# Full-array transposes of the probabilities, and the scores between the output runs, in a two-layer graph network

## The reference

```python
x = layernorm(x + (adj @ x) @ weight + bias)              # layer 0, for every batch
q, k, v = split(x @ w_qkv)                                # layer 1: 8 heads of 64
attn = softmax(where(adj == 0, -inf, q @ k.T * 64**-0.5))
o = (attn @ v) @ w_proj + b_proj
x = layernorm(x + o + layernorm(o) * gamma + beta)
```

## Time and profile before

| | before |
|---|---|
| three runs, median | 3365.83 us |
| profiled execution, its own time | 3366.38 us |
| its span in the profile | 3364.6 us |
| layer 0 | start to some 780 us |
| layer 1, fill in every group | some 840 to 3290 us |
| last pairs and last projection | some 3290 us to the end |
| TensorE busy in the span | 3308.5 us (98%) |

### The profile page before, as it was taken

The page is one execution under the profiler, slowest core; times in us unless marked ns, Lnnn a source line. Parts: engine busy times, 40 slices in busy tenths (PEclk is TensorE's granted clock), DMA queues, the critical chain, the costliest instruction groups (busy, mean ns, idle before and its releaser), DMA issues. The chain is left out here.

```text
span 3364.6 us, 88016 instructions
## 1 busy us (share of the span) xinstructions
PE 3308.5 (98%) x31792; PEld 2923.1 (87%) x31792; DVE 2623.7 (78%) x6434; ACT 2229.6 (66%) x4634; POOL 1997.1 (59%) x2690
## 2 busy tenths in 40 slices
PE   8999999998999999999999999999999999999996
PEld 6888888886899998889899899899999899998894
DVE  7666666665788888888888888888888888888887
ACT  4444444444677777777777777777777777777775
POOL 4555556552466666666666666666666666666666
PEclk8999999998999999999999999999999999999998
DMA  5565555653011111111122211111111111111210
GB/s 188 174 195 168 186 187 172 190 180 102 27 52 51 55 54 51 51 55 51 51 63 66 66 51 51 51 51 51 51 54 54 51 51 54 51 51 53 70 59 32
DMA packets 345217, 279.62 MB, mean 83 GB/s; under 512 B 13713, under 2 KB 275857, under 8 KB 344977
## 3 DMA queue, kind: packets, MB, share of 16 engines
q1 hardware_dynamic: 344976, 275.83, 27.0%
HBM read 141.56 MB, written 134.22 MB: 82 GB/s over the span
## 5 line engine op out<-in xcount | busy, mean ns | idle before, releaser
L1126 ACT ACTIVATE pt_hi<-bank 128x512 fp32r<-128x512 f32 x1024 | 557.0, 596 | 546.3 <-PE bank L835 533.9
L1119 ACT ACTIVATE probs<-probs,bias_row 128x512 f32<-128x512 f32 x1024 | 731.7, 721 | 44.7 <-DVE bias_row L1239 43.6
L1259 DVE TENSOR_TENSOR pt_lo<-bank,pt_hi 128x512 fp32r<-128x512 f32 x1024 | 658.0, 684 | 44.0 <-PE bank L858 34.3
L721 POOL TENSOR_SCALAR probs<-probs,inv_sums 128x480 f32<-128x480 f32 (+1 forms) x1024 | 685.3, 682 | 0.0
L1239 DVE CUSTOM_DVE_ANT_0 probs<-bank,mask_bias 128x512 f32<-128x512 f32 x1024 | 661.9, 684 | 9.7 <-PE bank L819 5.8
L718 POOL TENSOR_TENSOR probs<-probs,inv_sums 128x32 f32<-128x32 f32 x512 | 122.7, 240 | 730.4 <-DVE inv_sums L1248 730.3
L872 PE MATMUL bank<-x_lo,w_hi 64*128 64x512 f32 x1024 | 403.3, 394 | 0.0
L870 PE MATMUL bank<-x_lo,w_hi 64*128 64x512 f32 x1024 | 403.3, 394 | 0.0
L872 PE MATMUL bank<-x_hi,w_hi 64*128 64x512 f32 x992 | 403.2, 406 | 0.0
L870 PE MATMUL bank<-x_hi,w_hi 64*128 64x512 f32 x992 | 401.6, 405 | 0.0
L835 PEld LDWEIGHTS bank<-ident,probs 64*128 64x128 f32 x8192 | 362.9, 139 | 40.8 <-issue 4.9
(11 more groups left out here) (139 smaller groups left out, 10847.2 us busy)
## 6 DMA issues: line engine op xcount, KB each, us to landing
x_in<-in_x_dram SPq DMA_DIRECT2D x32, 1024.0 KB, 5.2
u_beta_rows<-ub SPq DMA_DIRECT2D x32, 1024.0 KB, 4.4
ut_hi<-ut_hi_sb SPq DMA_DIRECT2D x128, 256.0 KB, 4.1
ut_lo<-ut_lo_sb SPq DMA_DIRECT2D x128, 256.0 KB, 3.8
x_lo<-ut_lo SPq DMA_DIRECT2D x128, 256.0 KB, 4.7
out_dram<-o SPq DMA_DIRECT2D x128, 256.0 KB, 3.2
ub_row<-u_beta_rows SPq DMA_DIRECT2D x124, 256.0 KB, 2.7
x_hi<-ut_hi SPq DMA_DIRECT2D x124, 256.0 KB, 4.4
```

The source lines that it names most:

```text
L721: pool.tensor_scalar(probs[:, k % 2, a, cols], probs[:, k % 2, a, cols], inv_sums[:, k % 4, a:a + 1], 0.0, ALU.mult, ALU.add)\
L1119: act.activation(probs[:, k % 2, a, :], probs[:, k % 2, a, :], ACT.Exp, bias=bias_row[:, k % 4, a:a + 1], scale=-1.0, accum_out=sums[:, k ...
L1126: act.activation(turned_into(pt_hi, k, i), turned(i), ACT.Copy).then_inc(pthi_made, 1)
L1259: dve.tensor_tensor(turned_into(pt_lo, k, i), turned(i), f32(turned_into(pt_hi, k, i)), ALU.subtract).then_inc(ptlo_made, 1)
```

## The change

The transposes take all 128 rows: one for each head and each block of 128 keys, eight in a turn. Each takes 128 x 128 of `probs` as the weights and the 128 x 128 identity as the moving operand. Head a now lands in bank a, so that the views of the banks change, and ACT waits for each bank by itself. In the fourth step eight couples of fill stand ahead of run 0, and the scores stand between the two runs. The first step has six couples of fill at its end, and the second step 18 in place of 20. The number of fill couples in a group stays 48.

```diff
             def turned(i):
-                return t_bank[i][:].rearrange("p (a m n) -> p a m n", a=2, m=T)
+                return t_bank[i][:].rearrange("p (m n) -> p m n", m=T)
             def turned_into(rows, k, i):
-                first = k % T * P + i * HEAD
-                return rows[:, :, :, first:first + HEAD]
+                return rows[:, i, :, k % T * P:(k % T + 1) * P]
...
                     for a in range(2):
                         for m in range(T):
-                            for i, h in enumerate((TOP, BOTTOM)):
-                                cols = slice((a * T + m) * HEAD, (a * T + m + 1) * HEAD)
-                                last = pe.transpose(t_bank[i][:, cols], probs[h, k % 2, a, m * P:(m + 1) * P],
-                                                    ident[h, h])
-                                if a == 1 and m == T - 1:
-                                    last.then_inc(probs_turned, 1)
+                            cols = slice(m * P, (m + 1) * P)
+                            last = pe.transpose(t_bank[a][:, cols], probs[:, k % 2, a, cols], ident[:])
+                            if m == T - 1:
+                                last.then_inc(probs_turned, 1)
...
first_step:
-                        fill_and_wait(group, 12, 4, k + 1)
+                        fill_and_wait(group, 12, 6, k + 1)
second_step:
-                            fill(group, 16, 10)
+                            fill(group, 18, 9)
                         scores_ahead(k)
-                        fill_and_wait(group, 26, 10, k + 1)
+                        fill_and_wait(group, 27, 9, k + 1)
last_step:
-                            fill(group + 1, 0, 6)
+                            fill(group + 1, 0, 8)
...
                         attend_v(b, group, pt_hi, 0)
-                        if more_fill:
-                            fill(group + 1, 6, 2)
+
+                        scores_ahead(k, turn_next=True)
                         attend_v(b, group, pt_hi, 1)
-                        scores_ahead(k, turn_next=True)
...
                 def pt_hi_part(b, k):
-                    act.wait_ge(probs_turned, b * 32 + (2 * k + 2))
                     for i in range(2):
+                        act.wait_ge(probs_turned, b * 32 + (2 * k + i + 1))
                         act.activation(turned_into(pt_hi, k, i), turned(i), ACT.Copy).then_inc(pthi_made, 1)
```

## The result

The changed kernel took 3669.25 us, median of four runs (3668.71 to 3669.60), against 3365.68 us for the kernel of before: ratio 1.0905, 95% interval 1.0889 to 1.0921, so 304 us slower. I had predicted 3696 us (3540 to 3775), 330 us slower.

What follows compares the result with a forecast made beforehand. TensorE's own stream was taken to set the time of layer 1. 3366.4 us, plus 343 for 512 longer turns, minus 13 for the stall ahead of run 0, gave 3696 us, range 3540 to 3775 us.

Steps and rivals of the forecast that it cites:

- What bounds the kernel: TensorE's own stream sets layer 1's time; whatever the change adds to this stream it adds to the time.
- The full-array transpose: In a turn: 0.11 us each, against 0.061 for a half-array couple; eight take 0.88 us, 0.39 more.
- Rival B: Full-array transposes go at a half-array couple's pace, 0.061 us: 3496 us; chance 0.06.
- The change of mode: Ahead of and behind each turn, going half to full array and back costs 0.28 us together.
- Rival A: The 0.28 us for the change of mode is hidden behind matmuls in flight: 3553 us; chance 0.12.
- Rival E: The change of mode costs twice as much, 0.56 us: 3839 us; chance 0.05.
- Number of turns: All 512 turns counted at 0.67 us more each, the few without fill at the end included: +343 us.
- Eight fills ahead of run 0: Two more fill couples than today's six hide the 0.11 us that TensorE's stream loses there: -13 us.
- ACT's earlier start: ACT may begin its first copy after four transposes, which helps only where TensorE waits: 0.
- The fill moved to the first step: Fill moved from the second step to the first, and no fill less: 0.
- The scores between the runs: Fourth step: same work, two waits 0.92 us earlier; the longer turn hides the earlier wait: 0.
- Rival D: Fourth step, cheap turn: ready_to_turn waits for pt_lo, some 0.3 us in three of four groups: 3381 us; chance 0.03.

Runs made afterwards that it cites:

- experiment 1: The full-array transposes alone on the kernel of before, TensorE's order as before: 3682.7 us, ratio 1.0945.
- experiment 6: The kernel of before with one full-array transpose more at the head of every turn: 3577.8 us, ratio 1.0633.
- experiment 7: The kernel of before with layer 0's turns made by 16 full-array transposes instead of 32 half-array ones: 3377.7 us, ratio 1.0038.
- experiment 3: The kernel of before with the changed order, half-array transposes, and the wait for the next turn at run 1's last couple: 3340.7 us, ratio 0.9927.
- experiment 5: The kernel of before with fill moved between first and second step alone (4, 10, 10 couples become 6, 9, 9): 3356.2 us, ratio 0.9973.
- experiment 2: The changed kernel's order alone, with the half-array transposes of the kernel of before: 3382.0 us, ratio 1.0051.
- experiment 4: The changed kernel with the wait for the next turn moved to the last couple of run 1: 3670.0 us, ratio 1.0907.

## Why the prediction was right, and where it was off

**What bounds the kernel: right.** Experiments 1, 6 and 7 add to TensorE's stream, and the time grows by what the timeline shows, within 20 us: 504 x 0.67 = 338 us for 318 measured, 504 x 0.41 = 207 for 213, and 31 x 0.41 = 12.7 for 12.7. Of the 20 us too much in the first, 14 are the stall ahead of run 0, which goes.

**The full-array transpose: right.** I took 0.11 us from the last records of line 152; it is 0.109. Rival B (0.061 us) is refuted. The 56 ns of the Trainium skill (TensorE: Matmul & The Clock Gate, Back-to-back issue gap) do not hold for these fp32 transposes either. The page gives that figure for a matmul by itself, and some 81 ns for a stream of weight loads and matmuls of 128 columns, which I had not set beside it; the measured 109 ns is above both.

**The change of mode: right.** It was taken from layer 0, in the other direction: a turn with 1.23 us in all. It has 1.68 - 0.46 = 1.22. Experiments 6 and 7 show the price apart from the transposes (0.30 and 0.35 us for two changes). Rivals A and E are refuted. The Trainium skill (TensorEngine Tiling (Array Packing), Key Properties) says that such a change drains TensorE; the trace agrees, with 0.32 us from the last matmul to the first transpose.

**Number of turns: 5 us too much.** I took all 512. The last eight steps have no fill; from turn 504 to turn 511 the kernel of before takes 35.7 us (3296.9 to 3332.6) and the changed one 35.3 (3600.5 to 3635.8). I had reasoned that a longer turn on the chain of waits counts in full, which would be 4.7 us over these seven distances. With the transposes alone (experiment 1) the same turns take 38.2 us (3611.9 to 3650.1), so the longer turn costs 2.5 us there, about half of that, and the new order takes it back. That ACT starts in the middle of the turn would explain the half; no run tests it.

**Eight fills ahead of run 0: the number right, the cause not needed.** The stall goes, and 13 us is its size. With the short turn the two couples hide it: experiment 3, which has them, is 15 us faster than experiment 5, which hasn't. But experiment 1 has six couples as before and no stall. With the full-array transposes ACT's copies start no later than before, while run 0 comes 0.67 us later. I had put ACT's earlier start at nothing; in this kernel it does the work, together with the longer turn, and the two couples add nothing to it. Where ACT waits for the end of the turn the stall stays, although the turn is 0.41 us longer (experiment 6). So the -13 us came out right in part by luck: the same stall is covered twice, and the cover that I named is not the one that was needed.

**The fill moved to the first step: wrong, at nothing.** I wrote that no fill less means 0. With the short turn it takes a stall of 0.09 us out of each group, 9 us measured (experiment 5); with the long turn half of that stall is gone already (experiment 1). The row for it, the idle time of line 870's weight loads, lay beside the one for run 0 that I read.

**The scores between the runs: right for this turn.** I said that the earlier wait is hidden by the longer turn alone. Experiments 2 to 4 show just this. Rival D's price, 3381 us with a short turn, was measured as 3382, and this nearness is luck. The place and the three groups of four were right, but the gap is 0.43 us and not 0.3 (some 12 us too little), and I had not counted the second stall that the order removes (9 us too much).

**The sum.** 504 x 0.67 = +338, less 14 for run 0, less 9 for the first step, gives 315; measured are 304. The rest of 11 us I can only point at. Four steps take 19.82 us before and 22.24 us after, so 2.42 more; 4 x 0.67 - 0.11 - 0.09 = 2.48, and 0.06 us a group are left, 8 us in all. In the changed kernel the couples are down to 0.227 us after five behind most turns, before after some ten. No run here tests what does this, so this part of the sum stays open. The range that I gave for my own case, 3640 to 3760, was added up too narrow: both of its lower bounds together give 3624, both upper ones 3773.

## What to carry to other kernels

Where TensorE has no gap, count the moving columns and the changes between half-array and full-array instructions, not the instructions: two half-array transposes at the same time move half as many columns in turn as one full-array one, and a short burst in another mode pays for the drain twice. A reordering has to be read by each wait that moves with it; here one wait, four couples too early, turned a gain of 24 us into a loss of 17. And a cover such as "the longer turn hides it" belongs to the combination: test each half of a change by itself.

## What the hardware showed that I had not expected

A stall of a tenth of a microsecond on TensorE is not in its matmul rows at all: the records are 0.39 us long and 0.23 us apart, and so they bridge it. The idle time of the weight loads with "issue" as its cause showed both stalls, at once and counted (123 and 104 times). Not every such row is a stall of the order, though. In the changed kernel the change into full-array mode stands there as well: from 860 to 3590 us the weight loads of line 833 were idle for 172.5 us in 490 times, 0.35 us before each turn. Full-array transposes between full-array matmuls begin with no gap at all (0.22 us behind the last matmul, experiment 7), where half-array ones had 0.32 us.
